# A graph network's final layer: its adjacency matrix and its features split into two float16 parts each

## The reference

```python
loop = arange(n); row, col = [row, loop], [col, loop]; ew = [edge_weight, ones(n)]
deg = segment_sum(ew, col); dinv = where(deg > 0, rsqrt(deg), 0)
def gcn_conv(x, W, b):
    h = x @ W
    return segment_sum(h[row] * (dinv[row] * ew * dinv[col])[:, None], col) + b
h = max(layernorm(x), 0)
h = relu(gcn_conv(h, W1, b1))
return x + log_softmax(gcn_conv(h, W2, b2), axis=1)
```

## Time and profile before

| what | value |
|---|---|
| median of 3 runs | 2668.38 us (2668.35 to 2670.84) |
| the profiled execution's own time | 2671.28 us |
| its span, first to last instruction | 2669.5 us |
| mean granted TensorE clock | 0.787 of full speed |
| busy: PE, PEld | 2247.4 us (84%), 2104.9 us (79%) |
| busy: DVE, ACT, POOL | 1639.3 us (61%), 1355.3 us (51%), 1112.4 us (42%) |
| final layer | 2330.3 to 2669.5 us |

### The profile page before, as it was taken

One profiled execution on the slowest core, in us unless ns is written; L12 is line 12 of the kernel. 1 busy time (PEld: TensorE's weight loads), 2 busy tenths in 40 slices (PEclk: granted clock), 3 DMA queues, 4 the chain that ended last, 5 costly groups with the idle time before them and its releaser, 6 DMA issues. The chain is left out here.

```text
span 2669.5 us, 55867 instructions
## 1 busy us (share of the span) xinstructions
PE 2247.4 (84%) x18268; PEld 2104.9 (79%) x18269; DVE 1639.3 (61%) x3181; ACT 1355.3 (51%) x2800; POOL 1112.4 (42%) x1222
## 2 busy tenths in 40 slices
PE   2989898689999999698887787788778748789998
PEld 1878788689999999587777777777777648679998
DVE  7988888764333335676656666656666564455465
ACT  1666666643333332265555555555555522267686
POOL 2666666300000000377777777777777702200000
PEclk6999999999999999655555555555555569879999
DMA  1444344400000001444444444444444361096281
GB/s 57 135 137 141 132 140 142 133 2 2 2 2 2 2 2 31 131 117 117 109 110 117 109 111 116 109 111 115 109 113 114 99 238 78 5 395 220 89 293 32
DMA packets 155980, 281.63 MB, mean 105 GB/s; under 512 B 73475, under 2 KB 123878, under 8 KB 150470
## 3 DMA queue, kind: packets, MB, share of 16 engines
q1 hardware_dynamic: 117158, 200.48, 22.9%
q0 software_dynamic: 38688, 79.28, 11.7%
HBM read 210.52 MB, written 69.15 MB: 105 GB/s over the span
## 5 line engine op out<-in xcount | busy, mean ns | idle before, releaser
L1255 POOL DMA_INDIRECT layer_R<-source_terms,layer_srcs x800 | 780.6, 976 | 243.7 <-issue 243.7
L1487 PE MATMUL layer_zp<-layer_right,layer_left 96*128 96x192 f32 x1342 | 477.0, 541 | 170.5 <-DVE layer_left L1274 167.9
L1487 PEld LDWEIGHTS layer_zp<-layer_right,layer_left 96*128 96x128 f32 x1342 | 409.6, 330 | 186.8 <-DVE layer_left L1274 179.4
L1021 PEld LDWEIGHTS layer_acc<-layer_U,graph_CT 128*128 128x128 f16 x6250 | 524.9, 97 | 31.6 <-ACT layer_U L950 22.1
L1021 PE MATMUL layer_acc<-layer_U,graph_CT 128*128 128x192 f16 (+1 forms) x6250 | 530.2, 246 | 22.8 <-ACT layer_U L950 20.8
L1508 PEld LDWEIGHTS layer_acc<-layer_hot,layer_G 128*98 128x98 f32 x1648 | 260.8, 263 | 108.9 <-DVE layer_aggT L1328 108.5
L1508 PE MATMUL layer_acc<-layer_hot,layer_G 128*98 128x32 f32 x1648 | 275.7, 334 | 48.0 <-DVE layer_aggT L1328 47.9
L2226 PE MATMUL layer_acc<-layer_V,layer_turn 128*128 128x96 f32 x2500 | 288.0, 278 | 0.7 <-issue 0.7
L2226 PEld LDWEIGHTS layer_acc<-layer_V,layer_turn 128*128 128x128 f32 x2500 | 286.1, 195 | 0.9 <-issue 0.9
L1433 ACT ACTIVATE layer_y<-layer_R 128x1152 f32<-128x1152 f32 x135 | 156.3, 1158 | 236.6 <-DVE layer_R L1302 236.6
L1302 DVE TENSOR_TENSOR layer_R<-layer_zp,layer_R 128x1152 f32<-128x1152 f32 x135 | 182.4, 1351 | 144.2 <-DMA layer_R<-source_terms,layer_srcs 144.0
(11 more groups left out here) (313 smaller groups left out, 3156.0 us busy)
## 6 DMA issues: line engine op xcount, KB each, us to landing
layer_ring<-W_blocks SPq DMA_DIRECT2D x41, 1600.0 KB, 8.4
W_blocks<-nodes_x SPq DMA_DIRECT2D x150, 200.0 KB, 1.9
layer_left<-in_attr SPq DMA_DIRECT2D x68, 384.0 KB
C_blocks<-build_Cblk SPq DMA_DIRECT2D x25, 800.0 KB, 3.4
layer_C<-C_blocks SPq DMA_DIRECT2D x25, 800.0 KB, 20.0
layer_R<-source_terms,layer_srcs POOLq DMA_INDIRECT x800
...
```

The lines of the kernel that those rows point to most:

```text
L1021: return pe.matmul(acc[:, k % RING, 0:columns], CT[:, t, k * P:(k + 1) * P], pairs[:, cur, t, 0:columns], start=(t == 0), stop=(t == NT - 1))
L1255: nc.gpsimd.indirect_dma_start(R[:, i, u, :], None, P_d, bass.IndirectOffsetOnAxis(ap=at_u, axis=0)).then_inc(s_R[i], 16)
L1487: pe.matmul(out[u], left[:, i, u * P:(u + 1) * P], right[:, i, :], start=(u % 2 == 0), stop=False, skip_group_check=True)
```

## The change

The matmuls of the final layer's aggregation become float16. To keep precision, each operand is split into a high and a low float16 part: high = float16(scale x value), low = float16(scale x value - high). The scales are powers of two, found on the chip from the largest magnitudes.

- **W.** For each use, ACT makes the high part of all 25 source tiles in one pass over 3200 values (`high`). DVE makes the low part of the source tiles 0 to 18 (KD = 19) in eight pieces of 19 x 16 values (`low_piece`). GpSimd makes the low part of the tiles 19 to 24 in two passes over 6 x 128 values: scale into `scaled_W`, then subtract the high part.
- **V.** It is scaled and split into U, whose columns 0 to 95 are the high part and 96 to 191 the low part; `highs` on ACT, `rests` on DVE, five pieces each. This needs V's largest magnitude first (`reach`, `largest`, `largest_row`, `powers`), with two small steps on PE (`bound`), once for W's scale and once for each convolution.
- **Matmuls.** For each source tile two float16 matmuls with 192 columns, one for each part of W, in place of one float32 matmul with 96. DVE adds both halves of the sum and V in two steps and then makes `h`, one step more than before.
- **Layout.** The evictions in `build_matrices` now write W by pairs of windows: 16 columns side by side for each source tile. `ring` holds runs of 16 floats, in 8 slots instead of 9.

```diff
@@ build_matrices, ScalarE
-                    nc.scalar.activation(Wtwo[r][:, u % 2 * WC:(u % 2 + 1) * WC], win[:, u % 4, WC:2 * WC], ACT.Copy).then_inc(s_evac, 1)
+                    nc.scalar.activation(Wtwo[r].rearrange("p (k w d) -> p w k d", w=2, d=WIN)[:, u % 2, :, :],
+                                         win[:, u % 4, WC:2 * WC].rearrange("p (d k) -> p k d", d=WIN),
+                                         ACT.Copy).then_inc(s_evac, 1)
@@ weighted_gcn
-    RW = 9
+    RW = 8
     RT = 3
-    KA = 16
+    KD = 19
...
-        ring = m.sb("ring", [P, RW, P, NT], F32)
-        turn = m.sb("turn", [P, RT, NT, P], F32)
+        ring = m.sb("ring", [P, RW, WPT // 2, NT, 2 * WIN], F32)
+        turn = m.sb("turn", [P, RT, NT, 2, P], F16)
+        U = m.sb("U", [P, NT, 2, D], F16)
+        ones = m.sb("ones", [1, P], F32)
+        scaled_W = m.sb("scaled_W", [P, NT - KD, P], F32)
...
+        def by_tile(s, k):
+            return ring[:, s, :, k, :].rearrange("p v k d -> p k v d")
+
+        def two(u, part, k):
+            return turn[:, u % RT, k, part, :].rearrange("p k (v d) -> p k v d", d=2 * WIN)
+
+        def pair(u, part, k, v):
+            return turn[:, u % RT, k, part, v * 2 * WIN:(v + 1) * 2 * WIN]
+
+        def low_made(eng, u):
+            eng.wait_ge(s_low2, 2 * u + 2)
+            eng.wait_ge(s_low, u + 1)
...
@@ SyncE
-                    sp.wait_ge(s_turn2, freed + 1)
-                sp.dma_start(ring[:, s, :, :].rearrange("p d k -> p (d k)"), W_d[j, :, :]).then_inc(s_W[s], 16)
+                    low_made(sp, freed)
+                sp.dma_start(ring[:, s, :, :, :].rearrange("p v k d -> p (v k d)"), W_d[j, :, :]).then_inc(s_W[s], 16)
@@ GpSimd
+            nc.gpsimd.memset(ones[:, :], 1.0).then_inc(s_c, 1)
+            k = slice(KD, NT)
+            for u, (j, s, load) in enumerate(uses):
+                pool.wait_ge(s_turn, u + 1)
+                if u:
+                    pool.wait_ge(s_low2, 2 * u)
+                nc.gpsimd.tensor_tensor(scaled_W[:, :, :].rearrange("p k (v d) -> p k v d", d=2 * WIN), by_tile(s, k),
+                                        scale[:, :].unsqueeze(2).unsqueeze(3).to_broadcast([P, NT - KD, WPT // 2, 2 * WIN]),
+                                        ALU.mult).then_inc(s_low2, 1)
+                pool.wait_ge(s_low2, 2 * u + 1)
+                nc.gpsimd.tensor_tensor(turn[:, u % RT, k, 1, :], scaled_W[:, :, :], turn[:, u % RT, k, 0, :],
+                                        ALU.subtract).then_inc(s_low2, 1)
@@ VectorE
-            def by_source(u):
+            def low_piece(u, v):
 
                 j, s, load = uses[u]
-                if load:
-                    dve.wait_ge(s_W[s], landed[u])
-                if u >= RT:
-                    dve.wait_ge(s_acc, u - RT + 1)
-                nc.vector.tensor_copy(turn[:, u % RT, KA:, :],
-                                      ring[:, s, :, KA:].rearrange("p d k -> p k d")).then_inc(s_turn2, 1)
-
...
+                k = slice(0, KD)
+                if v == 0:
+                    dve.wait_ge(s_turn, u + 1)
+                one = nc.vector.scalar_tensor_tensor(pair(u, 1, k, v), ring[:, s, v, k, :], scale[:, :], pair(u, 0, k, v),
+                                                     ALU.mult, ALU.subtract)
+                if v == WPT // 2 - 1:
+                    one.then_inc(s_low, 1)
...
+            def largest(n):
+
+                do(nc.vector.tensor_reduce(most[:, 5:6], wdeg[:, :] if n == 0 else most[:, 0:5], AX.X, ALU.max,
+                                           apply_absolute_value=True))
+                dve.sem_inc(s_big, 1)
+
+            def largest_row(n):
+
+                dve.wait_ge(s_pr, n * (NT + 2) + 1)
+                do(nc.vector.tensor_reduce(row[:, :], wide, AX.X, ALU.max))
+                dve.sem_inc(s_big, 1)
+
+            def powers(n):
+
+                dve.wait_ge(s_pr, n * (NT + 2) + 2)
+                do(nc.vector.tensor_scalar(most[:, 5:6], spread, TINY, None, ALU.max))
+                do(nc.vector.tensor_scalar(bits[:, :], most[:, 5:6].bitcast(I32), MANTISSA, None, ALU.logical_shift_right))
...
+                if n == 0:
+                    do(nc.vector.tensor_tensor(scale[:, :], unscale[:, :], up[:, 0:1].bitcast(F32), ALU.mult))
+                dve.sem_inc(s_big, 1)
+                if n > 0:
+                    do(nc.vector.tensor_tensor(back[:, n - 1:n], down[:, 0:1].bitcast(F32), down[:, n:n + 1].bitcast(F32),
+                                               ALU.mult))
+
+            def reach(i, q):
+
+                t = slice(5 * q, 5 * q + 5)
+                dve.wait_ge(s_V, i * (NT + 5) + 5 * q + 5)
+                do(nc.vector.tensor_reduce(most[:, q:q + 1], V[:, i, t, :].rearrange("p t f -> p (t f)"), AX.X, ALU.max,
+                                           apply_absolute_value=True))
+
+            def rests(i):
+
+                largest(i + 1)
+                largest_row(i + 1)
+                powers(i + 1)
+                for q in range(5):
+                    t = slice(5 * q, 5 * q + 5)
+                    dve.wait_ge(s_hT, (i + 1) * NT + 5 * i + q + 1)
+                    nc.vector.scalar_tensor_tensor(U[:, t, 1, :], V[:, i, t, :], up[:, i + 1:i + 2].bitcast(F32), U[:, t, 0, :],
+                                                   ALU.mult, ALU.subtract).then_inc(s_V, 1)
...
-                if k >= KA:
-                    piece(0, k)
-            for u in range(1, RT):
-                by_source(u)
+                if k // (WPT // 2) < RT - 1:
+                    low_piece(k // (WPT // 2), k % (WPT // 2))
+                if k % 5 == 4 and k > 4:
+                    reach(0, k // 5 - 1)
+            reach(0, 4)
+            rests(0)
+            low(RT - 1)
...
-                    if base + n + RT < NL * NT:
-                        by_source(base + n + RT)
-                    if n == 0:
-                        dve.wait_ge(s_V, base + NT)
-                    do(nc.vector.scalar_tensor_tensor(part[:, n % 2, :], acc[:, n % 4, 0:D], unscale[:, :], V[:, i, j, :],
-                                                      ALU.mult, ALU.add))
-                    nc.vector.scalar_tensor_tensor(h[:, j, :], part[:, n % 2, :], dinv[:, j:j + 1], bias[:, i, :],
+                    do(nc.vector.scalar_tensor_tensor(part[:, n % 2, 0, :], acc[:, n % 4, D:2 * D], back[:, i:i + 1],
+                                                      V[:, i, j, :], ALU.mult, ALU.add))
+                    do(nc.vector.scalar_tensor_tensor(part[:, n % 2, 1, :], acc[:, n % 4, 0:D], back[:, i:i + 1],
+                                                      part[:, n % 2, 0, :], ALU.mult, ALU.add))
+                    nc.vector.scalar_tensor_tensor(h[:, j, :], part[:, n % 2, 1, :], dinv[:, j:j + 1], bias[:, i, :],
                                                    ALU.mult, ALU.add).then_inc(s_o, 1)
                     if i == 0 and n >= TURN + 1:
                         scaled(1, n - TURN - 1)
+                        if (n - TURN - 1) % 5 == 4 and n - TURN - 1 > 4:
+                            reach(1, (n - TURN - 1) // 5 - 1)
+                    if base + n + RT < NL * NT:
+                        low(base + n + RT)
@@ ScalarE
-                nc.scalar.activation(turn[:, u % RT, 0:KA, :], ring[:, s, :, 0:KA].rearrange("p d k -> p k d"),
-                                     ACT.Copy).then_inc(s_turn, 1)
-
...
+                k = slice(0, NT)
+                nc.scalar.activation(two(u, 0, k), by_tile(s, k), ACT.Copy, scale=scale[:, :]).then_inc(s_turn, 1)
+
+            def highs(i):
+
+                act.wait_ge(s_big, 3 * i + 7)
+                for q in range(5):
+                    t = slice(5 * q, 5 * q + 5)
+                    nc.scalar.activation(U[:, t, 0, :], V[:, i, t, :], ACT.Copy,
+                                         scale=up[:, i + 1:i + 2].bitcast(F32)).then_inc(s_hT, 1)
...
+            act.wait_ge(s_big, 3)
+            high(0)
+            act.wait_ge(s_var, 2)
+            nc.scalar.sqrt(stat[:, 2, :], stat[:, 1, :]).then_inc(s_root, 1)
+            high(1)
@@ TensorE
+            def bound(n):
+
+                pe.wait_ge(s_big, 3 * n + (2 if n else 1))
+                pe.transpose(wide, most[:, 5:6], ident[:, :]).then_inc(s_pr, 1)
+                pe.wait_ge(s_big, 3 * n + (3 if n else 2))
+                pe.matmul(spread, ones[:, :], row[:, :], start=True, stop=True).then_inc(s_pr, 1)
+
+            bound(0)
...
-                        if n == 0:
-                            pe.wait_ge(s_V, base + k + 1)
-                        mm = pe.matmul(acc[:, n % 4, 0:D], turn[:, (base + n) % RT, k, :], V[:, i, k, :],
-                                       start=(k == 0), stop=(k == NT - 1))
+                        if n == 0 and k % 5 == 0:
+                            pe.wait_ge(s_V, (i + 1) * NT + 5 * i + k // 5 + 1)
+                        for half in range(2):
```

(3 more changed lines are left out.)

85 lines of the change are left out of this document (47 added, 38 removed).

## The result

The changed kernel takes 2773.75 us, median of four runs (2767.84 to 2777.23), and the kernel before, measured beside it, 2669.36 (2668.35 to 2670.84): ratio 1.039, 95% interval 1.0374 to 1.0405. The prediction was 2801, between 2700 and 2860. The change makes the kernel slower by 104 us.

What follows compares the result with a forecast made beforehand. PE set the time before; VectorE, stalled by GpSimd, was to bound the loops after. 2671.28 + 116.5 (loops) + 16 (ahead of them) = 2803.8 us on the profiled scale, 2801 on the median's; range 2700 to 2860.

Steps and rivals of the forecast that it cites:

- ahead of the loops: Before the first aggregation: later layer norm +6, product stage +5, last reduction, power-of-two chain and first pieces of U +5; +16 us.
- first pieces and low parts of set 2: Loop start: four other pieces of `rests` 2.6, low parts 3.6 + 3.2; 9.4 us before VectorE takes the first sum.
- first convolution, 25 sets: 25 target tiles' low parts, each 5.0 us of VectorE work plus 3.0 of stall: 25 x 8.0 = 200 us.
- one set on PE: After the steps between the convolutions, PE's matmuls for one target tile, with nothing overlapping: 4.5 us.
- second convolution, 22 sets: 22 target tiles' low parts, each 5.7 us of VectorE work plus 2.8 of stall: 22 x 8.5 = 187 us.
- last set and its rows: End of the loops: the last target tile on PE 4.2 us, its rows 1.1.
- 3.2, minus 0.2: First convolution: VectorE waits up to 1.61 us for GpSimd twice a set, 3.2, less 0.2 beside unblocked work.
- by chance a fifth: Share of time GpSimd's passes lie beside unblocked VectorE work, 1.1 of 5.0 us; 0.2 off the first convolution's stall.
- The build: The 400 evictions of W that now rearrange columns were to cost 0; at 2 ns a value, 80 us of ScalarE.
- The clock rival (2819): Aggregation loops: TensorE's clock falls near 1.2 GHz, a set takes 8.7 us, 17 us more, 2819; chance 0.15.
- VectorE at half rate (2920): VectorE's low pieces run at half rate by the three-operand rule, 2.5 us more for each of 47 sets; chance 0.02.
- The rule of the shared interface: A VectorE instruction with two SBUF inputs and a GpSimd one reading SBUF: the second waits for the whole first; stall 3.2.

Runs made afterwards that it cites:

- one_pass_low: Changed kernel with W scaled by a constant 1/16 in the build, its low part one VectorE pass, GpSimd doing nothing: 2645.25 us, ratio 0.9901 to before.

## Why the prediction was right, and where it was off

**Direction and mechanism held.** VectorE became the bound, by blocking, as written: median piece 0.526, longest 1.92 where "about 0.5" and "near 2" stood. Blocking was inferred from the earlier trace rows; the two experiments that take away one reader each show it on both sides.

**The terms**, from the trace of the changed kernel:

| term | predicted | measured |
| --- | --- | --- |
| layer starts (varies from run to run) | 0 | -3.2 |
| ahead of the loops | +16 | +15.6 |
| first pieces and low parts of set 2 | 9.4 | 13.1 |
| first convolution, 25 sets | 200 (8.0) | 176.3 (7.05) |
| between the convolutions | 7.5 | 6.6 |
| one set on PE | 4.5 | 7.1 |
| second convolution, 22 sets | 187 (8.5) | 180.3 (8.19) |
| last set and its rows | 5.3 | 7.0 |
| loops in all, against 297.2 before | +116.5 | +93.2 |

The sum is -3.2 + 15.6 + 93.2 = 105.6, which is 2775.1 - 2669.5 of the two spans.

**The term that was mis-sized** is the first convolution, 23.7 of the 27 us that the forecast was too high. VectorE's own work was right: 5.0 predicted; 4.73, and 5.42 in each fifth set, so 4.87 on average. The step that failed is the stall, "3.2, minus 0.2": 7.05 - 4.87 = 2.2 measured. Three things make it smaller. Undisturbed passes take 1.47 and 1.64 us, 3.11 together, where the slope of the earlier trace rows had given 1.80 each. About 0.26 of each pass does not block, where 0.19 (1.80 - 1.61) had been taken. These two give 2.59 in place of 3.2. And what lies beside other work is 0.4 us a set on average, not 0.2. That was taken as "by chance a fifth", but it depends on when ScalarE's high copy ends. In eight of the 25 sets GpSimd starts as above, 0.06 us behind the start of `h`, waits for its end and then lies beside `scaled`: stall 2.37. In nine nothing is saved, pieces 6.24 and stall 2.59: in eight of these it starts behind the first piece, and in one no `scaled` stands behind `h`. In the others it starts earlier and holds up `h`, lies partly beside the reduction of V, or has no pass left to make. The head start is worth 0.2 us a set by the run that removed it.

The other terms are smaller and go both ways. The first row of the loops is 3.7 too low: VectorE waits 1.89 us for ScalarE's high copy of set 2, and a pass for set 3 falls on the same eight pieces, which take 8.95. Of the signs that the prediction gave, the longest piece near 2 us came true. PE waits 2.5 to 2.7 us behind a set at full clock in the first convolution and not 3 to 4, and the medians of the two passes, 1.51 and 1.75, lie under the 1.8 to 2.2.

**Second convolution**: 8.5 against 8.19, and for partly another reason. The forecast put the log-softmax in as work of VectorE, 1.2 us a set. The trace shows what it does to the order (ScalarE, then VectorE, then GpSimd):

```profile
2660.64 0.60 ACT L2282 ACTIVATE layer_ex<-layer_h 128x480 f32<-128x480 f32 x1 [9.40 <-DVEq L2106]
...
2662.66 8.65 ACT L2245 ACTIVATE layer_turn<-layer_ring,layer_scale 128x3200 f16<-128x3200 f32 x3
```

```profile
2665.65 11.52 DVE L2121 SCALAR_TENSOR_TENSOR layer_turn<-layer_ring,layer_scale,layer_turn 128x304 f16<-128x304 f32 x8 [1.26 <-ACT layer_turn L2245]
...
2665.69 1.47 POOL L2083 TENSOR_TENSOR layer_scaled_W<-layer_ring,layer_scale 128x768 f32<-128x768 f32 x1 [12.13 <-ACT layer_turn L2245]
...
2669.13 1.51 POOL L2083 TENSOR_TENSOR layer_scaled_W<-layer_ring,layer_scale 128x768 f32<-128x768 f32 x1
```

ScalarE waits 9.4 us before the exponential, and the high copies of three sets stand behind it in its stream. They then come in a row, and six passes of GpSimd in a row fall on the eight pieces of one set: 11.52 us, 7.9 of it stall. In the two sets that follow such a burst the pieces take 3.65, with no pass beside them. The clumps, which the prediction did not see, cost next to nothing: five sets take 41.1 us (2663.37 to 2704.47), and in the run in which GpSimd starts later, where there are no such bursts (four sets of 7.1 and one of 12.6), 41.0 (2601.16 to 2642.17).

**Ahead of the loops** the +16 was right in sum, not in its parts. The late layer norm is 9.5 us after the layer's start instead of 2.4, +7.2 against +6, because the last parameter transfer takes 4.96 rather than 3.8. 1.1 more is lost in L684, shown above, which the prediction had not placed there. The chains and the product stage together cost 7.3 where 10 stood. The ring with one slot less cost nothing, as written: in the loops nothing waits for its transfers.

**The build** cost nothing: L662, which now rearranges W's columns, still takes 339 ns, and L656 340, as in the earlier trace rows.

**The clock rival (2819)** came in part and changed little. Granted clock (the column behind POOL's, 1.00 is 2.4 GHz) in the first convolution before the change, then in one stretch of each convolution after it, then PE's rows around a slow set:

```profile
2391.00:2508.00 117.00, 117.00 (x1056) 117.00 (x1054) 63.08 (x80) 85.74 (x40) 0.00 (x0) 1.00 0.42 155
```

```profile
2440.00:2480.00 40.00, 28.27 (x310) 27.45 (x311) 39.54 (x70) 16.93 (x11) 18.12 (x11) 0.96 0.65 228
...
2640.00:2680.00 40.00, 23.62 (x245) 22.72 (x244) 37.41 (x58) 17.86 (x9) 16.43 (x10) 0.80 0.54 193
```

```profile
2469.26 5.94 PE L2333 MATMUL layer_acc<-layer_U,layer_turn 128*128 128x192 f16 x50 [2.51 <-DVE layer_turn L2121]
2476.34 3.87 PE L2333 MATMUL layer_acc<-layer_U,layer_turn 128*128 128x192 f16 x45 [0.84 <-DVE layer_turn L2121]
```

Before, PE was busy all the time in the loops and the clock 1.00 (2.4 GHz); now, after PE has waited for parts, it falls for stretches toward the lower level (1.2 GHz), to a mean of 0.80 in the second convolution. A slow set of matmuls lasts 1.65 us longer, PE then waits 0.84 instead of 2.51, and the next one starts on time. It costs only where VectorE waits for PE: in the first set of the second convolution (granted clock 0.59), 7.1 instead of 4.5, and in the last but one set (6.0 us at 0.70), which puts the last row of the loops at 7.0 instead of 5.3. Together that is 4 us, where the rival had 17 more.

**VectorE at half rate (2920)** fell: 304 values start 0.446 us apart with two float32/float16 SBUF operands, 400 values 0.546, so 1.04 ns a value and 0.13 fixed. The plain pass of one_pass_low, 1.09 ns a value (3.48/3200), is no faster. The Trainium skill ("Vector Engine (DVE) Microarchitecture Reference", Points that are easy to get wrong) would have it at half rate; these runs disagree. The rule of the shared interface that the prediction took from the Trainium skill ("SBUF — State Buffer", Who interferes with whom) holds in all runs above, with the part of each pass that does not block left over.
